# Moving part of the neighbour weighting and the norm squares from VectorE to ScalarE in a graph-transformer layer

## The chip, the cores and the metric

The kernel runs on one core of one Trainium2 chip. The metric is the device time of one execution in microseconds, as the median over runs. The kernel before takes 2964.49 us (three runs, 2961.64 to 2964.96).

## What is computed

The reference is one layer over 3125 nodes with 256 features: a layer norm, a graph attention over 103125 edges, a dense "mix" attention whose keys and queries are normalised per head, and a mixture-of-experts block. Two pieces of it matter here.

```
# graph attention: an edge's value row is weighted by its softmax weight, then summed by destination
m = v[src] * a[..., None]
ft2 = segment_sum(m, dst)
# mix attention: keys and queries are divided by their norm, head by head (8 heads of 32)
n = norm(t, axis=-1); t / maximum(n, 1e-12)
```

## The kernel before

The function `stage_edges_and_mix` does both attentions at once. It is the stage from about 250 to 1829 us of the profile.

**The edges.** They are sorted by destination and cut into 126 tiles of 128 rows with L = 8 slots each. GpSimd gathers the 8 slots of a tile (keys and values, 512 numbers a row) into `ring`, which holds four tiles; a gather for tile n starts only when both the weighing of tile n - 4 on VectorE (`val_ready`) and that on ScalarE (`act_val_ready`) are done. VectorE multiplies the keys with the query rows (`times_q`, L749, two halves), sums per head (`add_up`, L756), and makes the differences to the row maximum (`keep_own`, `top`, `less_top`). ScalarE takes the exponential (`exps`, L976). Then the values are weighted: slots 0 to 3 by one VectorE instruction (`weigh`, L777), slots 4 to 7 on ScalarE (`weigh_slot`, L983), which needs four ACTIVATEs a slot, one a head, since its scale is one number per row. VectorE adds the eight slots in three steps (`fold` L785, `fold_on` L790, `fold_last` L796). `fold` waits for both weighings.

**The order of a step.** The loop runs over n; each step has four micro steps, c = 0 to 3. VectorE's step n does, in this order: `times_q` of tile n (c = 0), `add_up` (c = 1), `keep_own`, `weigh` of tile n - 1, `top`, `less_top` (c = 2), and `fold` of tile n - 1, `compare`, `fold_on`, `settle`, `fold_last` (c = 3). ScalarE's step n does slot 5, 6 and 7 of tile n - 1 at c = 0, 1 and 2, and at c = 3 the exponentials of tile n and its slot 4. At the start of its step n, before slot 5, ScalarE issues the store of tile n - 2 and so waits for `fold_last` of that tile, which VectorE does at the end of step n - 1.

**The mix.** It is spread over the same micro steps by `micro_steps(n, c)`: a unit of 125 nodes takes nine micro steps, k = 0 to 8. First come 25 units of keys (K part, up to about 985 us), then some steps of coefficients, then 25 units of queries (Q part, about 1015 to 1745 us). In each micro step TensorE makes pair products (`kf`, L1085, or `qf`, L1141), ScalarE squares them (`phi`, L1015 or L1018, in `mix_first`, ahead of its weighing), TensorE multiplies the squares (L1095 or L1158), and in the K part VectorE adds the result to `g_acc` (L837). Because four micro steps make a tile and nine a unit, the pattern repeats every 9 tiles, which hold 4 units; k = 0 falls on c = 0, 1, 2 and 3 in turn. TensorE forms the query rows of the next tile (`q_of_rows`, L1059) at c = 1, and it needs the second `times_q` of the present tile to have read the old ones.

**A unit's norms.** At k = 0 of a unit VectorE squares the rows of the next one (`dve_square`, L516, stretch 0 of the micro step), sums them per head (`dve_sum`, L520, stretch 1) and scales and floors the sums (`dve_floor`, L525, stretch 2). ScalarE makes the root at k = 1 (`act_root`, Ln and Exp, L530 and L532). VectorE multiplies by the factor (`dve_grow`) and scales the rows (`dve_scale`) at k = 2. At k = 3 ScalarE rounds them (in the K part three ACTIVATEs), at k = 8 it copies the transposed parts out (L571). In the Q part VectorE divides the result of a unit (`divide`, L865) at k = 0, stretch 1; TensorE turns it (L1174) and ScalarE copies it (L1027), ahead of its weighing in that micro step.

The "stretches" of a micro step are the places between the edge instructions of VectorE where mix work is put. For c = 0 stretch 0 is ahead of both `times_q`, stretch 1 between them, stretch 2 behind them.

Of the kernel before, what the change touches and what calls it, by code (L numbers as in the profile page):

```python
# [26 lines left out]
ALU = mybir.AluOpType  # L27
ACT = mybir.ActivationFunctionType
# [34 lines left out]
AHEAD = 4  # L63
RING = 4
DROP = -1e30
COEF_MICRO = 9 * (NT + 1)
Q_MICRO = COEF_MICRO + 2
HW = HM // 2 * V1
# [30 lines left out]
def bcast(ap, *shape):  # L99
    return ap.broadcast_to(list(shape))  # L100
# [391 lines left out]
class Unit:  # L492
# [4 lines left out]
    def __init__(self, s, name, scratch, turn_ps, arrived, src, grow, factor):  # L497
        self.arrived, self.src, self.grow, self.factor, self.turn_ps = arrived, src, grow, factor, turn_ps
        self.sq, self.nrm, self.unit, self.rest, self.parts, self.turned_parts = scratch
        (self.order, self.squared, self.logged, self.rooted, self.scaled, self.rounded, self.rest_ready, self.middle, self.split,  # L500
         self.turned, self.ready) = (s.sem(f"{name}_{x}") for x in (
             "order", "squared", "logged", "rooted", "scaled", "rounded", "rest_ready", "middle", "split", "turned", "ready"))
# [8 lines left out]
        return ap.rearrange("p (h d) -> p h d", h=HM)  # L511


    def dve_square(self, dve, u):
        self.arrived(dve, u)
        dve.tensor_tensor(self.sq[u % 2][:, :], self.src(u), self.src(u), ALU.mult).then_inc(self.order, 1)  # L516

    def dve_sum(self, dve, u):
        dve.wait_ge(self.order, u * 3 + 1)
        dve.tensor_reduce(self.nrm[u % 2][:, 0, :], self.heads(self.sq[u % 2][:, :]), AX.X, ALU.add).then_inc(self.order, 1)  # L520

    def dve_floor(self, dve, u):

        dve.wait_ge(self.order, u * 3 + 2)
        dve.tensor_scalar(self.nrm[u % 2][:, 1, :], self.nrm[u % 2][:, 0, :], self.grow, 1e-24, ALU.mult, ALU.max  # L525
                          ).then_inc(self.squared, 1)

# [8 lines left out]
        dve.tensor_tensor(self.nrm[u % 2][:, 4, :], self.nrm[u % 2][:, 3, :], self.factor, ALU.mult).then_inc(self.order, 1)  # L536

    def dve_scale(self, dve, u):
        dve.wait_ge(self.order, u * 3 + 3)
        dve.tensor_tensor(self.heads(self.unit[u % 2][:, :]), self.heads(self.src(u)),  # L540
                          bcast(self.nrm[u % 2][:, 4, :].unsqueeze(2), TP, HM, DM), ALU.mult).then_inc(self.scaled, 1)

# [35 lines left out]
def micro_steps(n, c):  # L578

    i = 4 * n + c  # L580
    if i < COEF_MICRO:
        u, k = divmod(i, 9)
        return [("k", u - 1, k)]
    out = [("coef", 0, i - COEF_MICRO)] if i < COEF_MICRO + HM + 2 else []
    u, k = divmod(i - Q_MICRO, 9)
    if 0 <= u <= NT:
        out.append(("q", u - 1, k))
    elif u > NT:
        out.append(("end", 0, i - Q_MICRO - 9 * (NT + 1)))
    return out  # L590
# [3 lines left out]
def stage_edges_and_mix(nc, a, t):  # L594
    x = t.mix
    with Memory(nc) as s:
# [127 lines left out]
        def _(dve):  # L724
# [49 lines left out]

            def weigh(n):
                dve.wait_ge(exp_ready, n + 1)
                dve.tensor_tensor(val[n % 2][:, 0:L // 2, :, 0:DG],  # L777
                                  ring[:, n % RING, 0:L // 2, F:2 * F].rearrange("p s (h d) -> p s h d", h=HG),
                                  bcast(val[n % 2][:, 0:L // 2, :, DG:DG + 1], 128, L // 2, HG, DG), ALU.mult).then_inc(val_ready, 1)

            def fold(n):
                v = val[n % 2][:, :, :, :].rearrange("p s h d -> p s (h d)")
# [22 lines left out]
                    dve.tensor_tensor(t.x_all[:, u, :], late_ps[:, 0:F], t.late_bias[:, 2 * F:3 * F], ALU.add).then_inc(late_read, 1)  # L805

            def unit_first(unit, u, k):
                if u + 1 < NT and k == 0:
                    unit.dve_square(dve, u + 1)
                elif u + 1 < NT and k == 2:  # L810
                    unit.dve_grow(dve, u + 1)

            def unit_then(unit, u, k):
                if u + 1 < NT and k == 0:
                    unit.dve_sum(dve, u + 1)
                elif u + 1 < NT and k == 4:
                    unit.dve_rest(dve, u + 1)
                elif u + 1 < NT and k == 6:
                    unit.dve_last(dve, u + 1)

            def unit_last(unit, u, k):
                if u + 1 < NT and k == 0:
                    unit.dve_floor(dve, u + 1)
                elif u + 1 < NT and k == 2:
                    unit.dve_scale(dve, u + 1)

# [142 lines left out]
        @block.scalar  # L969
        def _(act):  # L970
            act.preload_act_table_set("natural_log_exp_and_others")

            def exps(n):
                act.wait_ge(less_ready, n + 1)
                wait(act, folded, n - 1)
                act.activation(val[n % 2][:, :, :, DG], less[n % 2][:, :, :], ACT.Exp, scale=1.0 / float(F) ** 0.5).then_inc(exp_ready, 1)  # L976

            def weigh_slot(n, e):

                act.wait_ge(exp_ready, n + 1)  # L980
                act.wait_ge(landed[n % RING * 2 + 1], 16 * (L // 2) * (n // RING + 1))
                for h in range(HG):
                    one = act.activation(val[n % 2][:, e, h, 0:DG], ring[:, n % RING, e, F + h * DG:F + (h + 1) * DG], ACT.Copy,  # L983
                                         scale=val[n % 2][:, e, h, DG:DG + 1])
                if e == L - 1:
                    one.then_inc(act_val_ready, 1)

            def keep_part(n):
                act.wait_ge(folded, n + 1)
                act.dma_start(t.parts[n * 128:(n + 1) * 128, :], part[n % 3][:, :]).then_inc(part_out[n % 3], 16)  # L990

            def unit_steps(unit, u, k):
                if u + 1 < NT and k == 1:
                    unit.act_root(act, u + 1)
                elif u + 1 < NT and k == 3:
                    if unit is k_:
                        act.wait_ge(late_read, (u + 1) * 2 + 1)
                        act.activation(v1[(u + 1) % 2][:, :, 1:V1], kv[(u + 1) % 2][:, F:2 * F].rearrange("p (h d) -> p h d", h=HM),
                                       ACT.Copy, scale=1.0 / N).then_inc(v1_ready, 1)
                    unit.act_round(act, u + 1)  # L1000
                    if unit is k_:
                        act.activation(ksq[(u + 1) % 2][:, :], k_.unit[(u + 1) % 2][:, :], ACT.Square).then_inc(ksq_ready, 1)
                elif u + 1 < NT and k == 5:
                    unit.act_middle(act, u + 1)
                elif u + 1 < NT and k == 8:
                    unit.act_turn_out(act, u + 1)
                    if unit is q_:
                        act.activation(qT[(u + 1) % 2][:, 0, :, :], qT_ps, ACT.Square)
                        act.activation(qT[(u + 1) % 2][:, 1, :, :], qT_ps, ACT.Copy).then_inc(qT_ready, 1)

            def mix_first(n, c):
                for kind, u, k in micro_steps(n, c):
                    if kind == "k" and u >= 0 and k < HM:
                        act.wait_ge(kf_ready, u * HM + k + 1)
                        act.activation(phi_k[k % 2], kf_ps[k % 2], ACT.Square).then_inc(kphi_ready, 1)  # L1015
                    elif kind == "q" and u >= 0 and k < HM:
                        act.wait_ge(qf_ready, u * HM + k + 1)
                        act.activation(phi_q[k % 2], qf_ps[k % 2], ACT.Square).then_inc(qphi_ready, 1)  # L1018

            def mix_last(n, c):  # L1020
                for kind, u, k in micro_steps(n, c):
                    if kind in "kq":
                        unit_steps(q_ if kind == "q" else k_, u, k)
                    if (kind == "q" and k == 0 and u > 0) or (kind == "end" and k == 0):
                        of = u - 1 if kind == "q" else NT - 1
                        act.wait_ge(yT_turned, of + 1)
                        act.activation(yT[of % 2], yT_ps, ACT.Copy).then_inc(yT_ready, 1)  # L1027

            for n in range(TILES + 2):
                for c in range(4):  # L1030
                    mix_first(n, c)
                    if c == 0 and n > 1:
                        keep_part(n - 2)
                    if c == 3 and n < TILES:
                        exps(n)
                    mix_last(n, c)
                    if c == 3 and n < TILES:
                        weigh_slot(n, L // 2)
                    elif c < 3 and 0 < n <= TILES:
                        weigh_slot(n - 1, L // 2 + 1 + c)  # L1040
            for j in range(3):
                act.wait_ge(part_out[j], 16 * len(range(j, TILES, 3)))

# [1078 lines left out]
```

## Time and profile before

| | us |
|---|---|
| median of the runs | 2964.49 |
| the profiled execution, its own time | 2960.23 |
| its span | 2958.4 |
| TensorE, VectorE, ScalarE, GpSimd busy over the span | 2249.8, 1903.7, 1119.8, 1335.2 |
| mean granted TensorE clock, share of full speed | 0.666 |

The profile is one execution; times in it are microseconds from the start of its span. PE is TensorE, DVE VectorE, ACT ScalarE, POOL GpSimd. In square brackets stands how long an engine sat idle ahead of an instruction and what ended that wait.

### The profile page before, as it was taken

To read this page: it belongs to the slowest core of one execution; us is meant where nothing else is said; L and a number is where in the kernel's file an instruction comes from. 1 tells how busy PE (TensorE), PEld (TensorE's weight loads), DVE (VectorE), ACT (ScalarE), POOL (GpSimd) and SP (SyncE) were. 2 spreads that over 40 slices of the span, in tenths; PEclk is the share of its full clock that TensorE was granted. 3 is DMA by queue.
4 is the path that set the end of the run, shared out by engine and by line. 5 is a ranking of instruction groups with operands and counts; after the bars stand their busy time and mean duration, and the time that the engine had idled before them with its cause. 6 is when DMAs were issued, how large, how long until landed. Compare 5 with 4: busy or idle time off the path is not lost. (4 is left out here: it accounts for less than half of the span.)

```text
span 2958.4 us, 41395 instructions
## 1 busy us (share of the span) xinstructions
PE 2249.8 (76%) x10483; PEld 1807.0 (61%) x10483; DVE 1903.7 (64%) x4402; ACT 1119.8 (38%) x3683; POOL 1335.2 (45%) x1284
## 2 busy tenths in 40 slices
PE   1273888888888889889899861677599805999996
PEld 1132666676666778788788750222288705888885
DVE  1454998998999987788788788444399841111121
ACT  0012565555555555555556553000155301222221
POOL 0004776776776766666666674333100052222222
PEclk7586665665655555555555555555599957999998
DMA  2135766666666766666666675222230044666664
GB/s 85 57 127 172 209 190 188 192 195 181 194 194 193 215 182 190 186 189 190 186 198 187 182 209 157 61 67 66 87 130 0 1 149 128 199 193 195 193 186 127
DMA packets 255430, 460.85 MB, mean 156 GB/s; under 512 B 49315, under 2 KB 174519, under 8 KB 255041
## 3 DMA queue, kind: packets, MB, share of 16 engines
q0 software_dynamic: 96256, 279.21, 33.4%
q1 hardware_dynamic: 137683, 159.50, 17.2%
q10 hardware_dynamic: 21294, 19.98, 2.0%
q8 instruction: 67, 1.10, 0.1%
q14 instruction: 130, 1.06, 0.1%
HBM read 400.32 MB, written 61.40 MB: 156 GB/s over the span
## 5 line engine op out<-in xcount | busy, mean ns | idle before, releaser
L679 POOL DMA_INDIRECT ring<-kv_tab,idx x1008 | 1072.0, 1064 | 690.4 <-issue 298.4
L983 ACT ACTIVATE val<-ring,val 128x64 f32<-128x64 f32 x2016 | 529.2, 337 | 57.0 <-DVE part L796 52.9
L749 DVE TENSOR_TENSOR prod<-ring,q_ps 128x1024 f32<-128x1024 f32 x252 | 301.4, 1214 | 1.7 <-DMA ring<-kv_tab,idx 1.7
L756 DVE TENSOR_REDUCE score<-prod 128x16 f32<-128x1024 f32 x252 | 300.6, 1211 | 0.0
L1911 POOL DMA_INDIRECT x_sum<-e_yw,to x64 | 99.7, 1557 | 379.3 <-DVE e_yw L1946 202.3
L1059 PE MATMUL q_ps<-q_win,spread 128*128 128x256 f32 x252 | 141.7, 663 | 155.5 <-DVE prod L749 154.8
L1942 DVE TENSOR_TENSOR e_y<-e_yps,e_b 128x512 f32<-128x512 f32 x32 | 22.1, 692 | 337.6 <-PE e_yps L2006 337.6
L1272 PE MATMUL step_ps<-scaled,hot 128*125 128x260 f32 x300 | 184.2, 717 | 71.7 <-DVE hot L1348 67.5
L1963 ACT ACTIVATE e_hT<-e_h,small 128x256 f32<-128x256 f32 x256 | 107.5, 471 | 341.6 <-PE e_h L1990 333.3
L785 DVE TENSOR_TENSOR val<-val 128x1040 f32<-128x1040 f32 x126 | 156.2, 1240 | 125.0 <-ACT val L983 124.4
L1990 PE MATMUL e_h<-e_xT,e_w 128*128 128x256 f32 x1024 | 228.9, 382 | 0.1
L2006 PE MATMUL e_yps<-e_w,e_hT 128*128 128x256 f32 x1024 | 226.3, 379 | 0.9 <-issue 0.9
L2006 PEld LDWEIGHTS e_yps<-e_w,e_hT 128*128 128x128 f32 x1024 | 194.5, 190 | 27.7 <-issue 1.3
L1990 PEld LDWEIGHTS e_h<-e_xT,e_w 128*128 128x128 f32 x1024 | 193.9, 192 | 26.0 <-issue 0.4
L1833 POOL DMA_INDIRECT x_rows<-rows,s_idx x50 | 60.5, 1210 | 289.3 <-DVE s_idx L1820 277.5
L1272 PEld LDWEIGHTS step_ps<-scaled,hot 128*125 128x125 f32 x300 | 74.2, 309 | 181.3 <-DVE hot L1348 177.3
L1158 PEld LDWEIGHTS bank_g<-g_acc,phi 124*125 124x125 f32 x800 | 178.4, 325 | 4.2 <-ACT phi L1018 0.9
L1158 PEld LDWEIGHTS bank_g<-g_acc,xn_buf 124*125 124x125 f32 x800 | 176.5, 321 | 4.7
L1059 PEld LDWEIGHTS q_ps<-q_win,spread 128*128 128x128 f32 x252 | 62.2, 303 | 191.1 <-issue 190.8
L1158 PE MATMUL bank_g<-g_acc,phi 124*125 124x33 f32 x800 | 175.9, 384 | 0.3
L1158 PE MATMUL bank_g<-g_acc,xn_buf 124*125 124x33 f32 x800 | 174.9, 382 | 0.0
L1095 PEld LDWEIGHTS bank_g<-v,phi 125*124 125x124 f32 x800 | 143.2, 265 | 46.9 <-DVE g_acc L837 27.6
(328 smaller groups left out, 4372.7 us busy)
## 6 DMA issues: line engine op xcount, KB each, us to landing
e_w<-L_ffn_W SPq DMA_DIRECT2D x64, 1024.0 KB, 5.2
parts<-part ACTq DMA_DIRECT2D x126, 130.0 KB, 3.5
loaded<-parts SPq DMA_DIRECT2D x126, 130.0 KB, 2.0
ring<-kv_tab,idx POOLq DMA_INDIRECT x1008, 3.8
q_win<-q_tab SPq DMA_DIRECT2D x126, 128.0 KB
x_rows<-g_ring SPq DMA_DIRECT2D x16, 516.0 KB
xr<-x_rows SPq DMA_DIRECT2D x32, 258.0 KB, 5.4
kv_tab<-kv_t SPq DMA_DIRECT2D x25, 250.0 KB
```

What stands on the lines that cost most here:

```text
L679: pool.indirect_dma_start(out=ring[:, n % RING, e, :], out_offset=None, in_=t.kv_tab, in_offset=bass.IndirectOffsetOnAxis(ap=idx[n % 6][:, ...
L749: dve.tensor_tensor(prod[half][:, :, :], ring[:, n % RING, at, 0:F], bcast(q_ps[:, 0:F].unsqueeze(1), 128, L // 2, F), ALU.mult).then_inc( ...
L756: dve.tensor_reduce(score[:, at, :], prod[half][:, :, :].rearrange("p s (h d) -> p s h d", h=HG), AX.X, ALU.add).then_inc(reduced, 1)
L785: dve.tensor_tensor(v[:, 0:4, :], v[:, 0:4, :], v[:, 4:8, :], ALU.add).then_inc(folding, 1)
L983: one = act.activation(val[n % 2][:, e, h, 0:DG], ring[:, n % RING, e, F + h * DG:F + (h + 1) * DG], ACT.Copy, scale=val[n % 2][:, e, h, D ...
L1059: pe.matmul(q_ps[:, 0:F], spread[n % 6][:, :], q_win[n % 3][:, :], start=True, stop=True).then_inc(q_ready, 1)
L1095: mm = pe.matmul(g_ps[h % 2][:, b, :], phi_k[h % 2][:, b * PB:(b + 1) * PB], v1[u % 2][:, h, :], start=True, stop=True)
L1158: mm = pe.matmul(y_ps[:, h, :], phi_q[h % 2][:, b, :], x.g_acc[:, h, b, :], start=False, stop=(b == NPB - 1), skip_group_check=True)
L1272: pe.matmul(step_ps[n % 2][:, 0:FD], hot[n % 2][:, :], scaled[n % 2][:, :], start=True, stop=True).then_inc(step_ready, 1)
L1963: gelu = act.activation(hT[par][:, b, :], h_ps[:, b, :], ACT.Gelu, bias=small[par][:, b:b + 1])
L1990: mm = pe.matmul(h_ps[:, b, :], w1[par][:, k, b * 128:(b + 1) * 128], xT[par][:, k, :], start=(k == 0), stop=(k == FC - 1))
L2006: mm = pe.matmul(y_ps[:, half, 0:F], hT[par][:, b, half * 128:(half + 1) * 128], w2[par][:, b, :], start=(b == 0), stop=(b == HB - 1))
```

## The change

ScalarE weighs six slots of a tile instead of four, and VectorE two (slots 0 and 1). ScalarE's slots come in four portions: slots 3 and 4 at c = 0, 5 and 6 at c = 1, 7 at c = 2, and slot 2 at c = 3 right behind the exponentials. The squares of a unit move to ScalarE, to the head of its micro step k = 0, ahead of the pair squares. On VectorE the sum of the squares moves from stretch 1 to stretch 2 of k = 0, and the floor from stretch 2 of k = 0 to stretch 0 of k = 1.

```diff
+V_SLOTS = 2
+A_SLOTS = ((3, 4), (5, 6), (7,), (2,))
...
-    def dve_square(self, dve, u):
-        self.arrived(dve, u)
-        dve.tensor_tensor(self.sq[u % 2][:, :], self.src(u), self.src(u), ALU.mult).then_inc(self.order, 1)
+    def act_square(self, act, u):
+        self.arrived(act, u)
+        act.activation(self.sq[u % 2][:, :], self.src(u), ACT.Square).then_inc(self.sq_ready, 1)
 
     def dve_sum(self, dve, u):
-        dve.wait_ge(self.order, u * 3 + 1)
+        dve.wait_ge(self.sq_ready, u + 1)
...
             def weigh(n):
                 dve.wait_ge(exp_ready, n + 1)
-                dve.tensor_tensor(val[n % 2][:, 0:L // 2, :, 0:DG],
-                                  ring[:, n % RING, 0:L // 2, F:2 * F].rearrange("p s (h d) -> p s h d", h=HG),
-                                  bcast(val[n % 2][:, 0:L // 2, :, DG:DG + 1], 128, L // 2, HG, DG), ALU.mult).then_inc(val_ready, 1)
+                dve.tensor_tensor(val[n % 2][:, 0:V_SLOTS, :, 0:DG],
+                                  ring[:, n % RING, 0:V_SLOTS, F:2 * F].rearrange("p s (h d) -> p s h d", h=HG),
+                                  bcast(val[n % 2][:, 0:V_SLOTS, :, DG:DG + 1], 128, V_SLOTS, HG, DG), ALU.mult).then_inc(val_ready, 1)
...
             def unit_first(unit, u, k):
-                if u + 1 < NT and k == 0:
-                    unit.dve_square(dve, u + 1)
+                if u + 1 < NT and k == 1:
+                    unit.dve_floor(dve, u + 1)
...
             def unit_then(unit, u, k):
-                if u + 1 < NT and k == 0:
-                    unit.dve_sum(dve, u + 1)
-                elif u + 1 < NT and k == 4:
+                if u + 1 < NT and k == 4:
...
             def unit_last(unit, u, k):
                 if u + 1 < NT and k == 0:
-                    unit.dve_floor(dve, u + 1)
+                    unit.dve_sum(dve, u + 1)
...
             def weigh_slot(n, e):
-                act.wait_ge(landed[n % RING * 2 + 1], 16 * (L // 2) * (n // RING + 1))
+                act.wait_ge(landed[n % RING * 2 + e // (L // 2)], 16 * (L // 2) * (n // RING + 1))
...
             def mix_first(n, c):
                 for kind, u, k in micro_steps(n, c):
+                    if kind in "kq" and u + 1 < NT and k == 0:
+                        (q_ if kind == "q" else k_).act_square(act, u + 1)
...
-                    if c == 3 and n < TILES:
-                        weigh_slot(n, L // 2)
-                    elif c < 3 and 0 < n <= TILES:
-                        weigh_slot(n - 1, L // 2 + 1 + c)
+                    of = n if c == 3 else n - 1
+                    if 0 <= of < TILES:
+                        for e in A_SLOTS[c]:
+                            weigh_slot(of, e)
```

## Rows read from the trace of the kernel before

**Rows 1.** Windows of 200 us: busy by engine (instructions), granted clock, DMA share, GB/s
```profile
800.00:1000.00 200.00, 174.55 (x807) 138.71 (x807) 183.54 (x399) 112.32 (x375) 140.83 (x131) 0.59 0.67 195
...
1200.00:1400.00 200.00, 179.34 (x922) 163.34 (x922) 159.62 (x321) 112.12 (x370) 127.55 (x123) 0.51 0.64 188
```

**Rows 2.** Groups by line, 400 to 1000 us: busy, mean ns, idle before
```profile
L777 DVE TENSOR_TENSOR val<-ring,val 128x1024 f32<-128x1024 f32 x49 | 59.8, 1220 | 0.0
...
L785 DVE TENSOR_TENSOR val<-val 128x1040 f32<-128x1040 f32 x48 | 59.4, 1238 | 32.2 <-ACT val L983 31.7
```

**Rows 3.** Groups by line, 1100 to 1600 us
```profile
L785 DVE TENSOR_TENSOR val<-val 128x1040 f32<-128x1040 f32 x39 | 48.5, 1242 | 56.0 <-ACT val L983 56.0
...
L1018 ACT ACTIVATE phi<-bank_f 124x500 f32<-124x500 f32 x68 | 39.6, 582 | 107.2 <-PE bank_f L1141 105.9
```

**Rows 4.** Timeline of ScalarE: start, length, instruction, idle before
```profile
982.10 2.98 ACT L983 ACTIVATE val<-ring,val 128x64 f32<-128x64 f32 x12 [0.50 <-DVE part L796]
```

**Rows 5.** Timeline of all engines, K part, unit at c = 0
```profile
601.88 1.19 PE L1059 MATMUL q_ps<-q_win,spread 128*128 128x256 f32 x2 [2.18 <-DVE prod L749]
...
605.96 0.58 ACT L1015 ACTIVATE phi<-bank_f 125x496 f32<-125x496 f32 x1 [2.70 <-PE bank_f L1085]
...
607.59 1.24 DVE L785 TENSOR_TENSOR val<-val 128x1040 f32<-128x1040 f32 x1 [1.03 <-ACT val L983]
```

**Rows 6.** Timeline of ScalarE and of VectorE, K part, three other tiles
```profile
631.70 0.21 ACT L530 ACTIVATE u_nrm<-u_nrm 125x8 f32<-125x8 f32 x1 [0.86 <-DVE u_nrm L525]
632.05 1.05 ACT L983 ACTIVATE val<-ring,val 128x64 f32<-128x64 f32 x4
...
633.29 1.24 DVE L785 TENSOR_TENSOR val<-val 128x1040 f32<-128x1040 f32 x1
...
643.40 1.06 ACT L983 ACTIVATE val<-ring,val 128x64 f32<-128x64 f32 x4
...
645.09 1.24 DVE L785 TENSOR_TENSOR val<-val 128x1040 f32<-128x1040 f32 x1
...
663.31 0.58 ACT L1015 ACTIVATE xn_buf<-bank_f 125x496 f32<-125x496 f32 x1 [2.34 <-PE bank_f L1085]
...
666.13 1.05 ACT L983 ACTIVATE val<-ring,val 128x64 f32<-128x64 f32 x4
...
667.74 1.24 DVE L785 TENSOR_TENSOR val<-val 128x1040 f32<-128x1040 f32 x1
```

**Rows 7.** Timeline of VectorE, Q part, unit at c = 1
```profile
1251.46 0.37 DVE L516 TENSOR_TENSOR u_sq<-x_buf 125x256 f32<-125x256 f32 x1
1251.75 1.21 DVE L756 TENSOR_REDUCE score<-prod 128x16 f32<-128x1024 f32 x1
1252.88 0.41 DVE L520 TENSOR_REDUCE u_nrm<-u_sq 125x8 f32<-125x256 f32 x1
1253.21 0.42 DVE L865 TENSOR_TENSOR ksq<-bank_g,y_inv 125x256 f32<-125x256 f32 x1
```

**Rows 8.** Timeline of TensorE, Q part, the four units of one 9-tile pattern
```profile
1195.01 0.68 PE L1174 MATMUL bank_l<-ident,ksq 125*128 125x125 f32 x2 [3.08 <-DVE ksq L865]
...
1224.11 0.68 PE L1174 MATMUL bank_l<-ident,ksq 125*128 125x125 f32 x2 [1.71 <-DVE ksq L865]
...
1253.68 0.68 PE L1174 MATMUL bank_l<-ident,ksq 125*128 125x125 f32 x2 [0.74 <-DVE ksq L865]
...
1282.17 0.68 PE L1174 MATMUL bank_l<-ident,ksq 125*128 125x125 f32 x2 [1.97 <-DVE ksq L865]
```

**Rows 9.** Timelines of GpSimd, VectorE and ScalarE, the last tiles
```profile
1748.06 1.28 POOL L679 DMA_INDIRECT ring<-kv_tab,idx  x1 [1.35 <-ACT val L983]
...
1815.96 1.22 DVE L749 TENSOR_TENSOR prod<-ring,q_ps 128x1024 f32<-128x1024 f32 x1 [1.69 <-DMA ring<-kv_tab,idx]
...
1823.95 2.97 ACT L983 ACTIVATE val<-ring,val 128x64 f32<-128x64 f32 x12 [1.42 <-DVE part L796]
...
1827.03 1.24 DVE L785 TENSOR_TENSOR val<-val 128x1040 f32<-128x1040 f32 x1 [2.40 <-ACT val L983]
```

More of the change, by code:

```diff
@@ L499, in __init__ @@
         self.sq, self.nrm, self.unit, self.rest, self.parts, self.turned_parts = scratch
+        self.sq_ready = s.sem(f"{name}_sq_ready")
         (self.order, self.squared, self.logged, self.rooted, self.scaled, self.rounded, self.rest_ready, self.middle, self.split,
@@ L511, in heads @@
         return ap.rearrange("p (h d) -> p h d", h=HM)
-    def dve_square(self, dve, u):
-        self.arrived(dve, u)
-        dve.tensor_tensor(self.sq[u % 2][:, :], self.src(u), self.src(u), ALU.mult).then_inc(self.order, 1)
+    def act_square(self, act, u):
+        self.arrived(act, u)
+        act.activation(self.sq[u % 2][:, :], self.src(u), ACT.Square).then_inc(self.sq_ready, 1)
     def dve_sum(self, dve, u):
-        dve.wait_ge(self.order, u * 3 + 1)
+        dve.wait_ge(self.sq_ready, u + 1)
         dve.tensor_reduce(self.nrm[u % 2][:, 0, :], self.heads(self.sq[u % 2][:, :]), AX.X, ALU.add).then_inc(self.order, 1)
     def dve_floor(self, dve, u):
-        dve.wait_ge(self.order, u * 3 + 2)
+        dve.wait_ge(self.order, u * 2 + 1)
         dve.tensor_scalar(self.nrm[u % 2][:, 1, :], self.nrm[u % 2][:, 0, :], self.grow, 1e-24, ALU.mult, ALU.max
@@ L538, in dve_scale @@
     def dve_scale(self, dve, u):
-        dve.wait_ge(self.order, u * 3 + 3)
+        dve.wait_ge(self.order, u * 2 + 2)
         dve.tensor_tensor(self.heads(self.unit[u % 2][:, :]), self.heads(self.src(u)),
```

## The prediction

> **What bounds the kernel now.** I read the windows first, to see which engine is full in the stage that the change touches. In the K part VectorE is busy 183.54 of 200 us and TensorE 174.55; in the Q part TensorE leads with 179.34 and VectorE falls to 159.62; ScalarE has 112 in both. TensorE's granted clock is 0.59 and 0.51 of full speed, so in the Q part it runs practically at the lower of its two levels, 1.2 GHz [rows 1]. Busy shares alone say "relieve VectorE". The groups by line say what VectorE's idle time is: it stands ahead of `fold` and ends with ScalarE's last weighing, 31.7 us over 48 tiles in the K part [rows 2] and 56.0 us over 39 tiles in the Q part [rows 3]. ScalarE in turn waits for TensorE: 107.2 us ahead of half of its pair squares [rows 3]. So I followed single tiles on the timelines. They form a ring: the second `times_q` lets TensorE form the next query rows, TensorE then does its products, ScalarE squares them at c = 2 and weighs slot 7 behind that, and then `fold` starts. One tile shows it whole: TensorE starts the query rows at 601.88 after waiting 2.18 us for VectorE, ScalarE gets its pair product at 605.96 after waiting 2.70, and `fold` starts at 607.59 after waiting 1.03 for slot 7 [rows 5]. In such a tile time taken from VectorE between `times_q` and `fold` turns into a longer wait at `fold`. `weigh` stands exactly there.
>
> **Removed from VectorE.** `weigh` halves. It takes 1.220 us for 1024 columns [rows 2]; half is 0.61, and since a VectorE instruction starts about 0.08 us before the end of the one ahead (0.37 long, next one 0.29 later [rows 7]), with the fixed part kept I take 0.53 a tile, 67 us over 126 tiles. The squares take 0.29 us from start to start [rows 7], 50 of them, 15 us. Upper bound of the gain if all of it lay on the path: 82 us. Lower bound of what it is worth: nothing, if `fold` waits in every tile.
>
> **Added to ScalarE.** A further slot costs a third of 2.98 us less the overlap: three slots in a row took 2.98 and one 1.05, so each further one 0.965 [rows 4, 6]. Two more a tile are 1.93 us, 243 us in all; the squares I price at 0.31 each, from VectorE's 0.29 and half of a 582 ns pair square of twice the width [rows 3, 7] (no row shows this ACTIVATE; a full 0.58 is the upper end, nothing the lower, where ScalarE waits for TensorE anyway). Busy time fits: 112 of 200 us become about 112 + 31 + 2 in the Q part, with 13 us a tile (39 tiles in 500 us [rows 3]). What decides is place. Between `fold_last` of one step and slot 7 of the next, ScalarE had three slots and now has five. This costs nothing where it idled 1.93 us there anyway, and moves slot 7, `fold` and the next tile where it did not.
>
> The Trainium skill speaks against this direction ("ScalarE: Activation LUTs", Rules for kernel authors: multiplications belong on VectorE). Four slots cost VectorE 1.22 us, and four cost ScalarE some 3.9 (2.98 and a further 0.965) [rows 2, 4], so the trace agrees on the price per element; by the rule alone the change would lose 1.4 us a tile, which holds only where ScalarE ends last. That case is the second rival.
>
> **K part, one pattern of 9 tiles.** In tiles of the kind of 607.59 the extra 1.93 us fits into the idle 2.70 [rows 5]. Here the unit's k = 0 is at c = 0, where square (about 0.34 in this part) and sum (0.33) stood ahead of the second `times_q`; both go from there, and since TensorE waited 2.18 for it, the ring gets 0.67 us shorter. Three kinds of tiles lose. At 633.29 `fold` did not wait; slot 7 ended at 633.10 and there was 0.86 us of idle time to absorb, so the new end is 633.10 + 1.93 - 0.86 + 0.3 for the square, near 634.5, and `fold` starts 1.2 later [rows 6]. At 645.09 nothing idles between the first portion and slot 7 (ended 644.46): 644.46 + 1.93 is 1.4 later than `fold` started [rows 6]. These two don't add: the second runs from TensorE's pair product, which is not delayed by the first except for some 0.35, and still has 0.67 in hand, so both together stand at 1.4 - 0.67 + 0.35 = +1.1. At 667.74 the first extra slot hides in 2.34 us of waiting and the second doesn't: 667.18 + 0.965 + 0.1, 0.5 later [rows 6]. The other five kinds absorb it. Sum of a pattern: +1.1 + 0.5 = +1.6, less 0.1 of old slack; six patterns: **+9 us**. Ends: 0, if the waits shift to cover it, and +19 if none of the three losses is shared (1.2 + 1.4 + 0.5 = 3.1 a pattern).
>
> **Q part, one pattern.** Every `fold` waits already [rows 3], so the cut in `weigh` is worthless in most tiles. But `divide` is due at k = 0, and TensorE waits for it in all four units of the pattern, 3.08, 1.71, 0.74 and 1.97 us [rows 8], and behind it runs without a wait for most of the tile. What stood ahead of `divide` counts. With the unit at c = 3 that is the sum alone, 0.33 (the square is covered by the wait at `fold`); at c = 0 and c = 1 square and sum, 0.29 + 0.33 = 0.62 each [rows 7]; at c = 2 also `weigh`, 0.62 + 0.53 = 1.15. Sum -2.7, each part less than TensorE's wait there. Against it stand ScalarE's extra slots: in most tiles it waits over 2 us for its pair products, 1.6 us for each one by the mean (107.2 / 68 [rows 3]); the tightest tiles come out even, and one that ends 0.65 later falls ahead of a stretch in which TensorE leads, so it isn't passed on. 25 units, 6.25 patterns: **-17 us**. Ends: -5 (ScalarE eats most) and -22.
>
> **Steps between and the last tiles.** In the four coefficient tiles VectorE has no pair squares to wait for and gains the 0.53 of `weigh` each, 2 in all; a tile on either side loses like those above, about 1 net: **-1**. In the last tiles, without mix work, VectorE would win 0.53 each, but GpSimd gathers without a ring wait from 1748.06 on, and VectorE waits 1.69 for the last gather at 1815.96 [rows 9]: no gain. At the very end ScalarE had three slots, 2.97 us, behind the last `fold_last` but one, with VectorE waiting 2.40 at 1827.03 [rows 9]; now it has five: +1.93, less 0.53 of `weigh`: **+1.4**. The floor, right behind the sum now, is due at k = 1; ScalarE's root may wait some tenths more, in a place that counts once a pattern at most; I leave it in the range. Ring and gathers: slot 7 still ends the tile, so gathers start when they did.
>
> **Sum.** +9 - 17 - 1 + 1.4 = -7.6 us against the profiled execution's 2960.23 (its span and 1.8 around it): 2952.6. The median of the runs stands 4.3 higher, so 2964.49 - 7.6 = about 2957.
>
> **Rivals.** (1) The two parts cancel, or the extra ScalarE work costs a little more in the K part (12 to 20 us): 2958.6 to 2970.4. For it speaks that the net is a difference of two small numbers. (2) Slower: ScalarE becomes the last in nearly every K tile, since its five slots behind `fold_last` leave no room for pair squares that come late. It decides from the point at which the three losing kinds stop sharing: 6 x 3.1 = 19 us, and with the Q part worth only -5, 2964.5 + 19 - 5 = about 2979. Against it: five of nine kinds idle 2 us or more. (3) VectorE counts fully: all 82 us, 2883; against it stand the waits at `fold`. A part of it, with losses in the K part near 0 and Q at -22, gives 2942. (4) It does nothing, since TensorE sets everything: 2965, inside the first rival; TensorE's waits for VectorE speak against it.
>
> **How the numbers follow.** A change under 0.2%, 5.9 us, can't be told from none. Forecast, -6 to -16 us: 0.40. Better than that, most of it the better ends of both parts: 0.12. Within 0.2%: 0.28. Slower: 0.20, shared by rival 2 and costs that I priced too low. Faster is 0.52. The range takes the better ends, 2940, and half way to rival 2, 2974; the likeliest case alone spans 2948 to 2958.5.
>
> **What would show it.** After the change VectorE's busy time should be 75 to 85 us lower and ScalarE's some 245 to 270 higher. VectorE's wait at `fold` for ScalarE should grow in both parts, by 0.5 to 1.5 us a tile. A 9-tile pattern of the K part should become some 1.6 us longer, one of the Q part 2.7 us shorter. TensorE's wait for `divide` should shrink. If the K pattern doesn't get longer, the losses at the three kinds of tiles are wrong; if the Q pattern doesn't get shorter, `divide` wasn't what TensorE's path hung on, or ScalarE's phi work delays TensorE, which would show as waits of TensorE for ScalarE that are hardly there now.

## The result and the profile after

The changed kernel takes 2969.39 us (median of 20 runs, 2961.67 to 2976.09) where the kernel before takes 2962.0 (20 runs): ratio 1.0023, 95% interval 1.0016 to 1.0031. It is slower by 7 us. The forecast was 7.6 us faster; the sign was wrong, though the time lies inside the range of 2940 to 2974. The profiled execution has a span of 2967.8 us, 9.4 more than before, so its parts below add up to 2 us more than the medians differ.

The engines' busy time, from the page of the changed kernel:

```profile
PE 2286.9 (77%) x10483; PEld 1843.2 (62%) x10483; DVE 1830.1 (62%) x4352; ACT 1362.2 (46%) x4741; POOL 1279.3 (43%) x1284
```

VectorE lost 73.6 us of work and ScalarE gained 242.4, each just short of what the prediction named as the sign (75 to 85 and 245 to 270). TensorE has the same 10483 matmuls as before and 37 us more busy time. Its granted clock fell from 0.59 to 0.57 in the first of these two windows, which answer to [rows 1]:

```profile
800.00:1000.00 200.00, 172.15 (x773) 136.47 (x773) 170.80 (x383) 143.27 (x508) 127.59 (x128) 0.57 0.65 191
...
1200.00:1400.00 200.00, 181.83 (x929) 165.07 (x929) 154.84 (x324) 144.29 (x512) 127.82 (x127) 0.51 0.65 191
```

Where the time went is best read by tile: the key part from the first `fold` to that of tile 53, the query part from tile 60 to 114. Windows of the kernel before and then of the changed one; the first number behind the bounds is the length, the third last one the granted clock:

```profile
285.00:945.60 660.60, 556.89 (x2595) 428.22 (x2594) 603.49 (x1316) 377.79 (x1252) 465.93 (x429) 0.62 0.66 193
1025.10:1721.50 696.40, 621.41 (x3194) 565.78 (x3194) 561.66 (x1124) 391.96 (x1300) 451.48 (x431) 0.51 0.64 189
```
```profile
290.00:967.00 677.00, 587.99 (x2596) 459.78 (x2594) 574.29 (x1292) 479.73 (x1700) 427.74 (x425) 0.58 0.64 187
1048.00:1731.40 683.40, 624.48 (x3191) 568.61 (x3192) 527.49 (x1099) 496.29 (x1755) 436.58 (x432) 0.51 0.65 192
```

The key part is 16.4 us longer, the query part 13.0 shorter. The first `fold` starts 5.0 us later (290.0 against 285.0). This delay is there already at the first `times_q` (275.06 against 270.04), ahead of any weighing, and in the other kernels below the first `fold` starts at 286.0 to 288.1; no term of the forecast stands for it, and it may be chance. The tiles between the parts cost 1.5, the last tiles 0.2 less. Together +9.7 up to the last `fold`, where the spans differ by 9.4.

VectorE's wait ahead of `fold` grew, as forecast: in the key part 58.0 us over 47 tiles where [rows 2] have 31.7 over 48, 0.6 a tile, and in the query part 70.2 over 39 where [rows 3] have 56.0, 0.4 a tile (forecast 0.5 to 1.5). In the key part `fold` waits in 48 of 53 tiles, where before it waited in 22. `weigh` now takes 0.685 us, 0.535 less. Groups by line of the changed kernel, 400 to 1000 us and 1100 to 1600 us:

```profile
L788 DVE TENSOR_TENSOR val<-val 128x1040 f32<-128x1040 f32 x47 | 58.4, 1242 | 58.5 <-ACT val L984 58.0
...
L780 DVE TENSOR_TENSOR val<-ring,val 128x512 f32<-128x512 f32 x48 | 32.9, 685 | 0.0
```
```profile
L788 DVE TENSOR_TENSOR val<-val 128x1040 f32<-128x1040 f32 x39 | 48.4, 1242 | 70.2 <-ACT val L984 70.2
```

The query part went as its step said. The turn of the divided result, the four units that answer to [rows 8]:

```profile
1183.44 0.68 PE L1177 MATMUL bank_l<-ident,ksq 125*128 125x125 f32 x2 [0.78 <-DVE ksq L866]
...
1213.11 0.68 PE L1177 MATMUL bank_l<-ident,ksq 125*128 125x125 f32 x2 [2.75 <-DVE ksq L866]
...
1241.00 0.68 PE L1177 MATMUL bank_l<-ident,ksq 125*128 125x125 f32 x2 [1.08 <-DVE ksq L866]
...
1269.91 0.68 PE L1177 MATMUL bank_l<-ident,ksq 125*128 125x125 f32 x2
```

The unit at c = 3 now waits 2.75 us for the division (3.08 before, less 0.33), the one at c = 0 1.08 (1.71 less 0.62), the one at c = 1 not at all (0.74 less 0.62), the one at c = 2 0.78 (1.97 less 1.15). These are the forecast cuts (0.33, 0.62, 0.62, 1.15) to about a tenth. TensorE's waits at this place sum up to 29.6 us where they were 46.0, over the stage.

The key part did not. The tiles that answer to [rows 6], from VectorE's timeline:

```profile
649.23 1.24 DVE L788 TENSOR_TENSOR val<-val 128x1040 f32<-128x1040 f32 x1 [0.86 <-ACT val L984]
662.30 1.24 DVE L788 TENSOR_TENSOR val<-val 128x1040 f32<-128x1040 f32 x1 [1.67 <-ACT val L984]
674.73 1.24 DVE L788 TENSOR_TENSOR val<-val 128x1040 f32<-128x1040 f32 x1 [0.87 <-ACT val L984]
686.75 1.24 DVE L788 TENSOR_TENSOR val<-val 128x1040 f32<-128x1040 f32 x1 [1.19 <-ACT val L984]
```

The three kinds named (first, second, fourth row) wait for slot 7 now, as forecast. But the third row's tile waits too, which was to absorb the load, and the step from the second to the third row is 12.43 us where it was 11.40. TensorE shows what goes with it. Its pair products, first before, then after, each from the one with which the second kind of tile begins:

```profile
638.20 0.62 PE L1085 MATMUL bank_f<-pair,u_T 96*125 96x496 bf16 x1
639.54 0.40 PE L1085 MATMUL bank_f<-pair,u_T 96*125 96x496 bf16 x1
...
649.15 1.05 PE L565 MATMUL turn_ps<-identb,u_parts 125*96 125x125 bf16 x8
```
```profile
653.25 0.62 PE L1088 MATMUL bank_f<-pair,u_T 96*125 96x496 bf16 x1
655.18 0.65 PE L1088 MATMUL bank_f<-pair,u_T 96*125 96x496 bf16 x1
...
668.90 1.05 PE L568 MATMUL turn_ps<-identb,u_parts 125*96 125x125 bf16 x8
```

Before, the second product takes 0.40 us, and from the first one to the unit's turn (L565, the transposition of its rows) TensorE needs 10.95 us; after, 0.65 us and 15.65 us for the same work. In that stretch the kernel before ran almost wholly at the higher clock level (granted clock 0.97) and the changed one at the lower (0.50), where TensorE is busy 15.20 of the 15.65 us.

Within the changed kernel the patterns of nine tiles come in two lengths, and the granted clock goes with them. Tiles 27 to 36 and 36 to 45, before and after:

```profile
622.50:735.20 112.70, 95.89 (x447) 73.73 (x446) 102.73 (x225) 64.20 (x213) 78.27 (x72) 0.62 0.65 190
735.20:847.90 112.70, 95.95 (x447) 73.72 (x446) 102.80 (x225) 64.22 (x213) 77.00 (x72) 0.62 0.66 190
```
```profile
637.60:753.80 116.20, 102.83 (x447) 79.82 (x446) 97.83 (x220) 81.41 (x289) 72.32 (x72) 0.57 0.63 185
753.80:867.20 113.40, 96.41 (x447) 74.93 (x446) 97.72 (x220) 81.29 (x289) 72.25 (x72) 0.62 0.65 189
```

At the clock of before, 0.62, a pattern takes 0.7 us more than before; the one at 0.57 takes 2.8 more on top. Of the five whole patterns four are of the long kind (115.4 to 116.3 us at 0.57).

That the low clock goes with the delay doesn't make it the cost of the change. The next lines are windows over two tiles, from the first to the second and from the second to the third of VectorE's rows above: before, in the changed kernel, and in that of the first experiment below, in which only the squares moved (with its whole pattern as the last line):

```profile
633.29:645.09 11.80, 10.91 (x54) 7.66 (x52) 11.77 (x28) 7.80 (x26) 9.36 (x9) 0.76 0.74 220
645.09:656.49 11.40, 8.72 (x52) 7.44 (x52) 11.40 (x28) 6.57 (x22) 8.96 (x9) 0.68 0.69 203
```
```profile
649.23:662.30 13.07, 12.62 (x45) 9.43 (x45) 11.34 (x25) 9.20 (x33) 8.45 (x8) 0.50 0.67 198
662.30:674.73 12.43, 12.43 (x57) 10.27 (x56) 10.99 (x26) 9.03 (x31) 8.01 (x8) 0.50 0.60 184
```
```profile
635.70:649.12 13.42, 13.42 (x50) 10.53 (x50) 11.88 (x28) 7.51 (x25) 8.49 (x9) 0.50 0.74 216
649.12:661.37 12.25, 12.25 (x56) 10.10 (x56) 11.34 (x26) 7.22 (x23) 8.36 (x8) 0.50 0.61 176
625.18:737.82 112.64, 104.92 (x447) 82.60 (x446) 101.86 (x221) 65.19 (x217) 74.92 (x72) 0.55 0.66 191
```

With no extra slot on ScalarE the same two tiles are as long at the lower level. (The last experiment on these chips has the same code in this part and shows them both ways: 13.42 and 12.24 us at 0.50, 12.05 and 11.31 at 0.72 and 0.71.) And yet the whole pattern stays at 112.6 us at a clock of 0.55, since its last tile, at 0.76, takes 12.95 us instead of 14.90. So these two tiles are long wherever TensorE is at the lower level, load or no load, but a low mean clock by itself doesn't make a pattern long. In the changed kernel, which has the load too, the last tile takes 14.91 us and doesn't make up for it.

### The profile page after: what moved, and what is told of

It reads as the page before. It is cut to its first block and busy times, and to the rows that moved or that the text cites. A ratio compares the mean times of both kernels' runs of the same rounds, so it can differ in the third digit from the quotient of the medians.

```text
span 2967.8 us, 42656 instructions
## 1 busy us (share of the span) xinstructions
PE 2286.9 (77%) x10483; PEld 1843.2 (62%) x10483; DVE 1830.1 (62%) x4352; ACT 1362.2 (46%) x4741; POOL 1279.3 (43%) x1284
## 5 line engine op out<-in xcount | busy, mean ns | idle before, releaser
L682 POOL DMA_INDIRECT ring<-kv_tab,idx x1008 | 1016.4, 1008 | 753.8 <-issue 290.4
L984 ACT ACTIVATE val<-ring,val 128x64 f32<-128x64 f32 x3024 | 770.0, 337 | 53.1 <-DVE part L799 48.8
L1098 PEld LDWEIGHTS bank_g<-v,phi 125*124 125x124 f32 x800 | 158.7, 291 | 44.1 <-DVE g_acc L838 24.0
```

Source lines behind the costliest of these rows:

```text
L682: pool.indirect_dma_start(out=ring[:, n % RING, e, :], out_offset=None, in_=t.kv_tab, in_offset=bass.IndirectOffsetOnAxis(ap=idx[n % 6][:, ...
L1098: mm = pe.matmul(g_ps[h % 2][:, b, :], phi_k[h % 2][:, b * PB:(b + 1) * PB], v1[u % 2][:, h, :], start=True, stop=True)
```

## The experiments

Theory A: the loss stands in the place of ScalarE's extra slots, behind the last `fold` of the tile ahead, and in the granted clock that goes with it; the query part's gain comes through the division. Rival B: the moved norm steps lose. Rival C: ScalarE's extra work costs wherever it stands. Rival D: VectorE is the bound. Three more came up on the way: E, three slots at c = 3 make TensorE wait for the next pair square; F, the short pattern is a matter of the data of its tiles; G, the loss needs the relief of VectorE as well.

One fact has to stand first. The experiments ran on five chips. On two of them the kernel before takes 2962 to 2965 us, as shown above. On three others it takes 3220 to 3263 us, and in the traces from there (none is of the kernel before) VectorE and ScalarE wait up to 14 us at a time with a releaser that the trace calls remote, mostly where they need a result of TensorE; the traces above have no such wait. I judge the theories by the first two chips, on which the time is that of the result, and tell of the others at the end. This choice was made after the first four kernels had run on one of the other three. Parts of the trace are compared with the one trace of the kernel before.

### Half of the change each, the relief alone, other portions

**Squares only** (weighing four and four, `e1b`; the edit is against the changed kernel):

```diff
-V_SLOTS = 2
-A_SLOTS = ((3, 4), (5, 6), (7,), (2,))
+V_SLOTS = 4
+A_SLOTS = ((5,), (6,), (7,), (4,))
```

> The kernel of e1_squares_only again, since the chip of the first four runs needed 3262 us for the kernel before where 2962 were shown, so that their differences don't bear on the 2962. Theory A: 12 to 18 us faster. Rival B: not faster.

Measured: 2953.05 us, ratio 0.9965 (0.9953 to 0.9978), 10 us faster. B falls; the gain is 2 us under A's range. Query part 9.5 us shorter (14 expected), key part only 0.9 (4 expected), at a clock of 0.57:

```profile
288.10:947.80 659.70, 590.70 (x2597) 463.13 (x2595) 598.40 (x1294) 383.09 (x1276) 445.97 (x427) 0.57 0.66 193
1026.90:1713.80 686.90, 627.38 (x3195) 572.04 (x3195) 556.28 (x1101) 399.21 (x1323) 458.24 (x432) 0.50 0.66 191
```

**Slots only** (`e2b`; the kernel before with the change's weighing, while squares, sum and floor stay as they were):

```diff
+V_SLOTS = 2
+A_SLOTS = ((3, 4), (5, 6), (7,), (2,))
...
-                    if c == 3 and n < TILES:
-                        weigh_slot(n, L // 2)
-                    elif c < 3 and 0 < n <= TILES:
-                        weigh_slot(n - 1, L // 2 + 1 + c)
+                    of = n if c == 3 else n - 1
+                    if 0 <= of < TILES:
+                        for e in A_SLOTS[c]:
+                            weigh_slot(of, e)
```

> The kernel of e2_slots_only again. Theory A: 15 to 22 us slower than before. Rival B: not slower.

Measured: 2981.44 us, ratio 1.0058 (1.0044 to 1.0071), 17 us slower. So the squares gain 10 and the slots lose 17, which adds up to the 7 of the whole. The key part carries it, 17.1 us, and the query part gains 2.8. Its patterns again have two lengths (third and fourth row, tiles 18 to 27 and 27 to 36):

```profile
286.80:964.50 677.70, 590.77 (x2597) 462.85 (x2596) 578.52 (x1316) 474.49 (x1676) 437.53 (x429) 0.58 0.65 188
1045.50:1739.10 693.60, 616.80 (x3193) 560.71 (x3193) 532.75 (x1123) 488.77 (x1732) 435.62 (x432) 0.51 0.65 190
518.70:635.00 116.30, 103.67 (x447) 81.43 (x446) 98.49 (x224) 80.89 (x285) 73.64 (x72) 0.56 0.64 184
635.00:747.00 112.00, 94.00 (x452) 72.50 (x451) 98.31 (x224) 80.19 (x286) 72.36 (x72) 0.65 0.66 192
```

The short pattern at a clock of 0.65 is even 0.7 us shorter than one before at 0.62, with the load in place. So the loss of this kernel stands in its long patterns alone, the ones with the low clock.

**Relief only** (`e5`; slots 2 and 3 are weighed by nobody and start at zero, so the sums are other numbers):

```diff
+V_SLOTS = 2
...
-                dve.tensor_tensor(val[n % 2][:, 0:L // 2, :, 0:DG],
+                dve.tensor_tensor(val[n % 2][:, 0:V_SLOTS, :, 0:DG],
...
+            for j in range(2):
+                dve.memset(val[j][:, V_SLOTS:L // 2, :, 0:DG], 0.0)
```

> VectorE weighs slots 0 and 1, ScalarE slots 4 to 7 as before, and nobody weighs slots 2 and 3 (their columns keep old sums): the relief of VectorE without the load on ScalarE. Squares as before. Theory A (weigh stands between the second times_q and the fold, where the ring over TensorE and ScalarE ends last): of 67 us taken from VectorE 5 to 12 come out, 2950 to 2957. Rival D (VectorE is the bound and the ScalarE load eats the gain): 30 us or more faster.

Measured: 2955.27 us, ratio 0.9961 (0.9949 to 0.9972), 11.6 us faster at the ratio. Some 66 us of VectorE's work are gone and a sixth of it comes out; D falls. VectorE's wait for slot 7 takes most of the rest: 157.8 us where the kernel before has 124.4, from 300 to 1900 us.

```profile
DVE val L786 <- ACT val L986: 157.8, 106, 3.0
```

**Load only, behind the fold** (`e6d`; the kernel before, with one more slot's work at c = 0 and at c = 1 into a buffer that nobody reads):

```diff
+        spent = [s.sb(f"spent{i}", [128, 2, HG, DG]) for i in range(2)]
...
+            def spend_slot(n, e, at):
+                for h in range(HG):
+                    act.activation(spent[n % 2][:, at, h, :], ring[:, n % RING, e, F + h * DG:F + (h + 1) * DG], ACT.Copy,
+                                   scale=val[n % 2][:, e, h, DG:DG + 1])
...
                     elif c < 3 and 0 < n <= TILES:
+                        if c < 2:
+                            spend_slot(n - 1, L // 2 + 1 + c, c)
                         weigh_slot(n - 1, L // 2 + 1 + c)
```

> The load alone behind the last fold (c = 0 and c = 1), fourth series. Where the kernel before takes about 2962 us, theory A (place): 15 to 25 us slower. Rival G (the loss needs the relief of VectorE too): under 6 us slower. Where it takes 3200 us or more: 0.4 to 0.8% faster, as in the three series before.

Measured: 2981.0 us, ratio 1.0068 (1.0055 to 1.0082), 20 us slower, as theory A said. Rival G falls: the load in that place makes the loss alone, without any relief of VectorE. Key part +12.8, query part +2.0, the tiles between them +2.1, the rest at both ends:

```profile
286.40:959.80 673.40, 575.38 (x2597) 449.86 (x2595) 604.52 (x1318) 473.77 (x1676) 465.97 (x429) 0.60 0.66 189
1041.40:1739.80 698.40, 624.68 (x3193) 568.92 (x3192) 561.42 (x1122) 489.87 (x1732) 453.00 (x432) 0.51 0.65 188
```

Its key patterns have the two lengths too: 112.1 and 112.2 us, no more than before, at a clock of 0.65, and 115.6 to 116.4 at 0.57 to 0.59.

**The same six slots in other portions** (`e3b`): three at c = 3, right behind the exponentials, where ScalarE is ahead, and one each at c = 0, 1 and 2 as before. The edit is against the changed kernel.

```diff
-A_SLOTS = ((3, 4), (5, 6), (7,), (2,))
+A_SLOTS = ((5,), (6,), (7,), (2, 3, 4))
```

> The kernel of e3_portions_early again (slots 2, 3, 4 at c = 3, one each at c = 0, 1, 2). Theory A (place behind the last fold decides): 15 to 25 us faster than before. Rival C (ScalarE's extra work costs wherever it stands): within 3 us of the changed kernel, 5 to 10 slower than before. Rival E (three slots at c = 3 delay the next pair square at c = 0, and TensorE waits for it; in the first series it was 1.8% slower): TensorE shows waits for ScalarE ahead of L1098 and the kernel is 10 us or more slower.

Measured: 2944.79 us, ratio 0.9938 (0.9924 to 0.9952), 18 us faster than before. ScalarE does the same work as in the changed kernel (busy 1355.2 us against 1362.2). C falls, and so does E on this chip: TensorE's waits for ScalarE are 16 us in the stage (11 before), none of them for a pair square. The key part is 9.7 us shorter than before, at a clock of 0.63, and the query part keeps its gain, 11.7:

```profile
286.00:936.90 650.90, 549.53 (x2597) 425.71 (x2596) 572.50 (x1294) 478.28 (x1700) 428.57 (x430) 0.63 0.68 196
1014.50:1699.20 684.70, 623.10 (x3195) 569.96 (x3195) 529.70 (x1100) 492.21 (x1755) 434.51 (x432) 0.51 0.66 192
```

On these two chips this is the fastest of the kernels tried.

**Six slots only in tiles 60 to 124, squares throughout** (`e4c`, against the changed kernel; VectorE weighs the other two or four):

```diff
+def a_slots(n, c):
+    return (((3, 4), (5, 6), (7,), (2,)) if Q_FIRST <= n < TILES - 1 else ((5,), (6,), (7,), (4,)))[c]
```

> Six slots on ScalarE only in tiles 60 to 124, squares moved throughout, third series. Where the kernel before takes about 2962 us, theory A: 12 to 16 us faster. Against it: within 3 us of squares-only, 10 us faster. Where it takes 3200 us or more: within 0.3% of before, as in the two series before.

Measured: 2949.37 us, ratio 0.9963 (0.995 to 0.9977), 11 us faster; the interval takes in both sides of that expectation. The query part has 684.8 us, that of squares only 686.9: there the six slots are worth 2 us. In the key part this kernel does just what squares only does, yet takes 657.5 us, 3.1 less than before, at a granted clock of 0.62 where squares only had 0.57:

```profile
286.80:944.30 657.50, 559.65 (x2597) 434.14 (x2596) 598.04 (x1293) 382.72 (x1276) 449.18 (x429) 0.62 0.67 194
```

So the squares are worth up to 3 us there, near the 4 expected, and without the load the lower clock goes with 2 us over the whole part, not with 3 a pattern.

### The chips on which the kernel before takes over 3200 us

The one new edit here is the load ahead of the fold: the work of the two spent slots is done at c = 3, right behind the exponentials (with waits for the exponentials and the gather inside `spend_slot`).

```diff
                     if c == 3 and n < TILES:
+                        for at in range(2):
+                            spend_slot(n, L // 2 + at, at)
                         weigh_slot(n, L // 2)
```

> Only the squares move to ScalarE, with the sum and the floor on VectorE in their new places; the weighing is split four and four as before. Theory A (the loss is in the place of the extra slots in the key part, and in the granted clock that falls there; the query part gains through the division): square and sum ahead of the division are worth 0.33 + 3 x 0.62 = 2.2 us a pattern in the query part, 14 us in all, and 0.7 a pattern in the key part, 4 us: 12 to 18 us faster than before, about 2947. Rival B (the moved norm steps make ScalarE and VectorE wait for each other and carry the loss): not faster than before, 2962 or more.

> Only the weighing moves, six slots on ScalarE in the four uneven portions; squares, sum and floor as before. Theory A: the query part keeps only the half of the weighing that stands ahead of the division in one unit of four, 0.5 us a pattern, 3 us in all; the key part loses what the changed kernel lost there and the 4 us that the squares gave, and the last tile 1.9: 15 to 22 us slower than before, about 2980. Rival B: the slots alone don't lose, 2962 or less.

> The changed kernel with the same six slots in other portions: slots 2, 3 and 4 at c = 3, and one each at c = 0, 1 and 2, so that behind the last fold ScalarE has three slots as before. Theory A (place): the key part no longer loses, the query part keeps its gain, the last tile loses nothing: 15 to 25 us faster than before, about 2943. Rival C (the extra ScalarE work costs wherever it stands, through its share of time or through memory): within 3 us of the changed kernel, 2966 to 2972.

> The changed kernel with six slots on ScalarE only for tiles 60 to 124 (query part and the plain tiles); tiles 0 to 59 and the last one are split four and four. Squares moved throughout. Theory A: the key part gains 4 us through the squares, the query part keeps 14 to 17: 15 to 22 us faster than before, about 2944. Rival B or C: the query part gave its gain for another reason and the total stays within 6 us of before.

> The kernel before, with the load alone: at c = 0 and at c = 1 ScalarE does one more slot's four ACTIVATEs into a buffer that nobody reads; VectorE weighs four slots as before. Theory A (place): the three kinds of key tiles lose as in the slots-only kernel and nothing is won anywhere; +17 there, +3 for what the query part won, +2 for the last tile as there: 15 to 25 us slower than before. Rival C: as slow as the same load at c = 3.

> The same load alone, both extra slots at c = 3 behind the exponentials. Theory A (place): ScalarE has idle time there, so 0 to 4 us slower than before. Rival C: 15 to 25 us slower, as e6_load_behind_fold.

> The kernel of e4_split_by_part again, on another chip if possible (squares moved throughout, six slots on ScalarE only in tiles 60 to 124). Theory A: squares-only gave 10 us; the query part of the changed kernel was 3.5 us shorter than that of squares-only, and the key part stays as with squares only: 12 to 16 us faster than before, about 2949. Against it: within 3 us of squares-only.

> The changed kernel again beside the others. Theory A: 5 to 9 us slower than before. Its key patterns come in two lengths again, 116.2 and 113.4 us, and the short ones have the higher granted clock; which of them are short may differ. Rival F (the short pattern at tile 36 is a matter of the data of those tiles): the same pattern is short again and no other.

Measured, each against the kernel before on the same chip, in four series. The second and third runs of the two loads carried the expectations of the first (15 to 25 us slower behind the fold, 0 to 4 ahead of it):

| kernel | ratio, 95% interval |
|---|---|
| squares only | 1.0021 (0.9987 to 1.0055) |
| slots only | 0.9918 (0.9888 to 0.9949) |
| portions early | 1.0176 (1.013 to 1.0222) |
| split by part, twice | 0.9982 (0.9952 to 1.0013), 0.9984 (0.9956 to 1.0013) |
| the changed kernel | 0.9983 (0.9952 to 1.0014) |
| load behind the fold, three times | 0.9941 (0.9914 to 0.9967), 0.9958 (0.9925 to 0.9992), 0.9923 (0.9893 to 0.9954) |
| load ahead of the fold, three times | 1.0105 (1.0073 to 1.0136), 1.0009 (0.9971 to 1.0047), 0.9984 (0.9949 to 1.0018) |

Nearly every expectation fails here, and partly turns round: pure extra work behind the fold makes the kernel 0.4 to 0.8% faster, three times over, and the portions that win on the other chips lose 1.8%. The load ahead of the fold is between 0.2% faster and 1.0% slower, so place matters here as well, but the other way round. Rival F has no answer: the changed kernel's key patterns take 121.6 to 136.1 us here, in no two lengths. Rival E may hold here: in the portions early TensorE waits 38.1 us for pair squares of the query part, of which the same kernel has none on the other chip. The waits of the third of the load-behind series, whole kernel:

```profile
ACT u_T L571 <- remote: 104.2, 22, 10.4
ACT phi L1021 <- remote: 71.7, 20, 9.0
ACT phi L1024 <- remote: 57.6, 16, 13.8
DVE y_inv L900 <- remote: 57.0, 11, 9.9
```

All four wait for a result of TensorE. What delays it there, and why work on ScalarE helps, no run here settles. Load ahead of the fold was run on these chips alone; that it would cost nothing on the others is argued from the portions early, not shown.

## Why the prediction was wrong

- **What bounds the kernel**: right on the chips of the result. A sixth of the relief comes out.
- **Removed and added work**: right, 0.535 us of `weigh` (0.53 forecast); 73.6 us in all (82 as the upper bound), 242.4 on ScalarE. The square, which no row had, takes 0.40 us there (0.31 forecast).
- **Query part, -17**: right in mechanism and sign, 13.0 measured; TensorE's waits at the division shrank by the forecast amounts. Of the six patterns, 1.5 to 3.4 us shorter, one reached the 2.7.
- **Key part, +9**: this is the step that failed, at +16.4. It took TensorE's times in every tile from the trace, and so its clock, as given, and let the tile from the second to the third row absorb the load. At the old clock the loss is under the forecast: a pattern costs 0.7 us more (1.6 said), the first two losing kinds 1.4 together (1.1), the last 0.2 (0.5), and the tile at c = 0 is 0.66 shorter, as the squares' 0.67 said. But four of five whole patterns ran at 0.57 and cost 2.8 us more on top. In them TensorE is at the lower level in the second and third tile of the pattern, comes to the unit's turn late, and the tile that was to absorb the load loses 1.03. That this loss is the load's own is not shown: it comes with the lower level in squares only too, where another tile makes up for it. (One small slip: 644.46 + 1.93 is 1.3 later than 645.09, not 1.4.)
- **Between and last tiles, -1 and +1.4**: +1.5 and -0.2. Why the tiles between got longer was not followed up; with the load alone they are 2.1 longer, with the portions early 1.8 shorter. The last `fold` waits 4.84 us where it waited 2.40 [rows 9], for five slots in 4.88 us, as forecast; the plain tiles gave back a little more than thought. Timelines of VectorE and ScalarE, the last tile:

```profile
1836.69 1.24 DVE L788 TENSOR_TENSOR val<-val 128x1040 f32<-128x1040 f32 x1 [4.84 <-ACT val L984]
```
```profile
1831.71 4.88 ACT L984 ACTIVATE val<-ring,val 128x64 f32<-128x64 f32 x20 [1.42 <-DVE part L799]
```

- **Direction**: a net of -7.6 out of +9 and -17 had no margin for an error of 7 in one term. And it wasn't one term alone: in the profiled execution the key part is off by 7.4, the query part by 4.0, the tiles between by 2.5, and 5.0 stand ahead of the stage's first `fold`, where nothing was forecast. That the time fell inside the range is no success of the mechanism. The numbers are those of the first rival (12 to 20 us lost in the key part, 2958.6 to 2970.4 in all), the mechanism in part that of the second: ScalarE came last in 48 of 53 key tiles, but the query part kept most of its gain. The Trainium skill's rule (ScalarE: Activation LUTs, Rules for kernel authors) would have given the sign, but not its reason: the same slots on ScalarE, moved within the step, win.

Open: why the granted clock differs between patterns of one kernel with the same matmuls. In the kernels with slots or load behind the fold the long patterns and the low clock come together (116.3 us at 0.56, 112.0 at 0.65 in slots only), and the rows don't tell which came first; in squares only a pattern at 0.55 is as long as one before at 0.62.

## What to carry to other kernels

Before work is moved to an engine with idle time, find the stretch between the two waits that tie this engine to the others and count what it must do in that stretch; with five of the six slots behind the last fold the whole change lost 7 us, and with three of them there it won 18. On one of the slower chips those winning portions lost 1.8%, so the trial belongs on the chip that counts. A part that gains and a part that loses should be tried apart: the squares alone won 10 us, and the slots lost 17. A sum of small terms of both signs is worth its direction only if it allows for what comes with TensorE's clock: patterns of one kernel, with the same matmuls, here differed by 3 to 4 us in 113.

## What the runs showed of the hardware that was not expected

- The granted clock of TensorE in the key part, at the same number of matmuls: 0.62 before, 0.57 with the squares moved, 0.58 in the changed kernel, 0.63 with the portions early. With slots behind the fold the long patterns are those with the low clock (116.3 us at 0.56, 112.0 at 0.65 in slots only); with the squares alone moved, 112.6 us at 0.55 is no longer than 112.7 at 0.62 before.
- The same instructions in the key part ran at 0.57 in 659.7 us and at 0.62 in 657.5 (squares only, and the kernel with six slots from tile 60 on).
- Chips differ by 9 to 10% on this kernel (2962 to 2965 us on two, 3220 to 3263 on three), and the sign of an edit of half a per cent can differ with them.
